# Six of 12.5 column blocks of an edge projection move from one stage to two others

## The reference, cut to what matters

```
x = x + L0_gnn(norm(x), src, dst, ...)          # stages gat_*: attention sums over edges
x = x + L0_ffn(norm(x), ...)                    # stages one_*: one of 32 experts a node
x = x + L1_gnn(norm(x), edge_attr_256, ...)     # stages edge_*

L1_gnn:  msg = (node_feats[src] + edge_feats) @ W1.T + b1
         s   = msg @ W4.T + b4 + (node_feats @ W5.T + b5)[dst]     # 8 heads
```

## Time and profile before

| | |
|---|---|
| median of 3 runs | 5361.3 us (5359.38 to 5363.87) |
| the profiled execution | 5358.89 us, its span 5357.1 us |
| mean granted TensorE clock | 0.835 of full speed |
| busy share of the span | PE 66%, DVE 55%, POOL 31%, ACT 17% |
| moved by DMA | 749.97 MB, mean 140 GB/s |

### The profile page before, as it was taken

How to read it: one execution, slowest core, us unless ns; L and a number is a source line. 1 busy time by engine, 2 the same in 40 slices (tenths; PEclk the granted TensorE clock), 3 DMA queues, 4 the chain that set the end, 5 groups by cost and what they waited for, 6 DMA issues and landing times. The chain is left out here.

```text
span 5357.1 us, 65064 instructions
## 1 busy us (share of the span) xinstructions
PE 3536.3 (66%) x17025; PEld 2564.0 (48%) x17039; DVE 2953.5 (55%) x6866; ACT 918.5 (17%) x2005; POOL 1660.0 (31%) x1548
## 2 busy tenths in 40 slices
PE   0583785364922776956679898989719636557359
PEld 0352553233511553733357686767518624345247
DVE  4696765324948977568841213030422258687657
ACT  0200001121000011204721213131304310000022
POOL 3376660224765850020010000000040246657200
PEclk9897897585965997979889898989759868879769
DMA  4276894243765970002366362626122226756200
GB/s 125 77 191 193 279 352 139 83 111 116 190 195 180 377 261 16 2 4 92 163 213 199 101 205 79 202 85 203 55 75 69 65 58 178 205 155 184 71 34 19
DMA packets 471878, 749.97 MB, mean 140 GB/s; under 512 B 70098, under 2 KB 343790, under 8 KB 467161
## 3 DMA queue, kind: packets, MB, share of 16 engines
q1 hardware_dynamic: 317021, 502.62, 28.4%
q0 software_dynamic: 82176, 177.60, 12.8%
q10 hardware_dynamic: 72436, 66.76, 3.7%
HBM read 593.67 MB, written 152.81 MB: 139 GB/s over the span
## 5 line engine op out<-in xcount | busy, mean ns | idle before, releaser
L883 PE MATMUL gin_up_sums<-gin_ring,gin_high 125*128 125x504 f32 (+1 forms) x1400 | 533.2, 381 | 32.6 <-PEq L184 32.6
L883 PE MATMUL gin_up_sums<-gin_ring,gin_low 125*128 125x504 f32 (+1 forms) x1400 | 524.4, 375 | 0.0
L863 DVE BATCH_NORM_STATS2 gin_up_stat<-gin_mlp_z 128x6 f32<-128x500 f32 (+1 forms) x112 | 70.1, 626 | 586.1 <-ACT gin_mlp_z L937 586.1
L2522 POOL IOTA two_seats_pid<- 125x1 f32 x1 | 0.1, 132 | 1145.7 <-ACTq L2519 1145.7
L883 PEld LDWEIGHTS gin_up_sums<-gin_ring,gin_high 125*128 125x128 f32 x1400 | 268.3, 192 | 74.3 <-issue 37.3
L883 PEld LDWEIGHTS gin_up_sums<-gin_ring,gin_low 125*128 125x128 f32 x1400 | 268.5, 192 | 40.5 <-issue 3.7
L3505 PE MATMUL adj_counts_part<-adj_counts_far,adj_counts_low 128*128 128x325 bf16 x1032 | 217.6, 342 | 103.3 <-DVE adj_counts_far L3481 43.3
L3134 PE MATMUL edge_sum_part<-edge_ring_rows,edge_sum_hot 128*125 x832 | 214.5, 407 | 64.2 <-DVE edge_sum_hot L1916 64.0
L3206 POOL DMA_INDIRECT edge_edge_held<-edge_table,src_e x204 | 212.6, 1042 | 105.9 <-issue 58.2
L3134 PE MATMUL loops_sum_part<-loops_ring_rows,loops_sum_hot 128*125 x832 | 212.0, 414 | 48.4 <-DVE loops_ring_rows L1495 44.6
L3134 PE MATMUL gat_sum_part<-gat_ring_rows,gat_sum_hot 128*125 x832 | 204.7, 400 | 18.8 <-issue 10.3
(11 more groups left out here) (863 smaller groups left out, 8102.1 us busy)
## 6 DMA issues: line engine op xcount, KB each, us to landing
gin_ring<-gin_adj SPq DMA_DIRECT2D x80, 1260.0 KB, 5.8
gin_ring<-gin_adj SPq DMA_DIRECT2D x60, 945.0 KB, 4.8
edge_own_rows<-edge_attr_quads_in SPq DMA_DIRECT2D x97, 512.0 KB, 12.3
gin_adj<-adj_counts_tile SPq DMA_DIRECT2D x25, 1575.0 KB
gat_sum_ef<-edge_attr_t_in SPq DMA_DIRECT2D x128, 256.0 KB
pre<-edge_edge_held ACTq DMA_DIRECT2D x204, 128.0 KB
edge_ring_rows<-pre SPq DMA_DIRECT2D x51, 512.0 KB
pre<-gat_gat_held ACTq DMA_DIRECT2D x144, 128.0 KB
```

What stands on the lines that cost most here:

```text
L863: v.bn_stats(stat[:, f, p * 6:(p + 1) * 6], z1[:, f, t0 * P:(t0 + n) * P]).then_inc(stats, 1)
L883: mm = pe.matmul(sums[h][k][:, 0:n * PC].rearrange("p (t n) -> p t n", n=PC), piece[:, t, k * 128:(k + 1) * 128], counts, start=(t == 0 an ...
L2522: pool.iota(pid[:], pattern=[[0, 1]], base=0, channel_multiplier=1, allow_small_or_imprecise_dtypes=True).then_inc(made, 1)
```

## The change

`gat_sum` keeps three of the six blocks of 512 columns and the rest: 24 full and 4 short steps in place of 48 and 4. They are spread over the 104 quads, one after three or four quads. The other 24 full steps go into a new class `OwnParts`: 12 into `one_send`, 12 into `one_back`. There SP loads a step's features (four buffers), PE multiplies, ACT takes each block of 256 columns out of PSUM and at the end writes 128 x 768 values to `edge_own`, and waits for that write. The edge features come in two arrays that are laid out so that a step is one transfer with 8 KB in one piece for each partition, in `gat_sum` too, in place of four transfers with pieces of 1 KB. The bytes stay the same.

```diff
+OWN_SENT, OWN_BACK = 3, 3
+OWN_EARLY = (OWN_SENT + OWN_BACK) * OWN_COLS // EDGE_COLS
...
+class OwnParts:
+    PLACES, HELD = RUNS // STRIPES, 4
...
+    def load(self, sp):
+
+        for n in range(self.steps):
+            if n >= self.HELD:
+                sp.wait_ge(self.projected, n - self.HELD + 1)
+            sp.dma_start(self.ef[n % self.HELD][:], self.feats[self.first * self.PLACES + n]).then_inc(self.loaded[n % self.HELD], 16)
+
+    def project(self, pe):
+
+        for n in range(self.steps):
+            b, place = n // self.PLACES, n % self.PLACES
+            low = (RUNS - 1 - place) * H
+            pe.wait_ge(self.loaded[n % self.HELD], 16 * (n // self.HELD + 1))
+            if place == 0 and b >= 2:
+                pe.wait_ge(self.put, b - 1)
+            for k in range(KD):
+                for m in range(STRIPES):
+                    mm = pe.matmul(self.bank[b % 2][m * 32:(m + 1) * 32, 0:OWN_COLS], self.g.edge_proj[:, k, low:low + 32],
+                                   self.ef[n % self.HELD][:, m, k, :], start=(place == 0 and k == 0), stop=(place == self.PLACES - 1 and k == KD - 1))
+            mm.then_inc(self.projected, 1)
+
+    def keep(self, act):
+
+        for b in range(self.count):
+            act.wait_ge(self.projected, (b + 1) * self.PLACES)
+            act.activation(self.kept[:, b, :], self.bank[b % 2][:, 0:OWN_COLS], ACT.Copy).then_inc(self.put, 1)
+        act.wait_ge(self.put, self.count)
+        lo = self.first * OWN_COLS
+        act.dma_start(self.g.edge_own[:, lo:lo + self.count * OWN_COLS], self.kept[:].rearrange("p b c -> p (b c)")).then_inc(self.out, 16)
+        act.wait_ge(self.out, 16)
...
-    QUADS, LEAD = RING // QUAD, 5
-    STEPS = LOOPS * PARTS + PLACES
...
+    QUADS, LEAD = S // QUAD, 5
+    LATE = LOOPS - OWN_EARLY
+    STEPS = LATE * PARTS + PLACES
+    end_of = [(n + 1) * QUADS // STEPS - 1 for n in range(STEPS)]
...
-                    for m in range(STRIPES):
-                        first = (m * PLACES + place) * RUN + b * EDGE_COLS + lo
-                        sp.dma_start(ef[n % HELD][:, m, :, 0:cols], ef_v[:, :, first:first + cols]).then_inc(ef_in[n % HELD], 16)
+                    late = feats[:, first:first + STRIPES * KD * cols].rearrange("p (m k c) -> p m k c", m=STRIPES, k=KD)
+                    sp.dma_start(ef[n % HELD][:, :, :, 0:cols], late).then_inc(ef_in[n % HELD], 16)
...
                 (sent,), (before,) = st2.gathers(1, top * T)
+                own = OwnParts(g, st2, early, 0, OWN_SENT) if early is not None else None
                 with st2.block() as block:
+                    if own is not None:
+                        @block.tensor
+                        def _(pe):
+                            own.project(pe)
+
+                        @block.scalar
+                        def _(act):
+                            own.keep(act)
...
                     @block.sync
                     def _(sp):
+                        if own is not None:
+                            own.load(sp)
                         sp.wait_ge(g.weights_in, g.weights_due)
                         sp.wait_ge(sent, before + 16 * top * T)
```

More of the change, by code:

```diff
@@ L1420, in _, with __init__ @@
                         q.then(v.tensor_scalar(mean[:], mean[:], 1.0 / H, None, ALU.mult))
+class OwnParts:
+    PLACES, HELD = RUNS // STRIPES, 4
+    def __init__(self, g, st, early, first, count):
+        self.g, self.first, self.count = g, first, count
+        self.steps = count * self.PLACES
+        self.feats = early.rearrange("p (n m k c) -> n p m k c", m=STRIPES, k=KD, c=OWN_COLS)
+        self.ef = [st.sb(f"own_ef{b}", [128, STRIPES, KD, OWN_COLS]) for b in range(self.HELD)]
+        self.kept = st.sb("own_kept", [128, count, OWN_COLS])
+        self.bank = [st.ps(f"own_bank{b}", [128, 512]) for b in range(2)]
+        self.loaded = st.sems("own_loaded", self.HELD)
+        self.projected, self.put, self.out = st.sem("own_projected"), st.sem("own_put"), st.sem("own_out")
+    def load(self, sp):
[23 more added lines that the diff above has]
+        act.wait_ge(self.out, 16)
 def sum_heads(nc, g, name, ring, weight, acc, ahead, edge=None, reload=None):
@@ L1524, in quad @@
                     n = (s + j) // QUAD
-                    if edge is not None and (n + 1) % spaced(n) == 0:
-                        project(step_at(n))
+                    if edge is not None and n in step_ending:
+                        project(step_ending[n])
                 pe.sem_inc(summed, HOTS)
@@ L1545, in _ @@
                 for n in range(S // QUAD):
-                    if edge is not None and n % spaced(n) == 0:
-                        load_feats(step_at(n))
+                    if edge is not None and n in step_starting:
+                        load_feats(step_starting[n])
                     c = (n + LEAD) * QUAD
@@ L1723, in gat @@
         acc = st0.sb("acc", [P, T, D + H])
[L1724 removed]
+        sum_heads(nc, g, "gat_sum", ring, weight, acc, ahead, (A["edge_attr_late"], g.edge_own, logit))
         with Stage(nc, g, "gat_out") as st:
@@ L2579, in _, with moe @@
                 q.then(v.tensor_copy(expert_of[:], expert_f[:]))
-def moe(nc, g, name, heads, bias, w1, b1_col, w2, b2, experts, hidden, top, relu):
+def moe(nc, g, name, heads, bias, w1, b1_col, w2, b2, experts, hidden, top, relu, early=None):
     HM = min(hidden, 128)
@@ L2773, in _, with seats_back @@
                     second(s)
-def seats_back(nc, g, name, seat, share, results, top, relu):
+def seats_back(nc, g, name, seat, share, results, top, relu, early):
     PLACES = 8
@@ L2783, in seats_back, with _ @@
         rows_in, before = st.gathers(PLACES, [len(order[j::PLACES]) for j in range(PLACES)])
+        own = OwnParts(g, st, early, OWN_SENT, OWN_BACK) if early is not None else None
         with st.block() as block:
+            if own is not None:
+                @block.sync
+                def _(sp):
+                    own.load(sp)
+                @block.tensor
+                def _(pe):
+                    own.project(pe)
+                @block.scalar
+                def _(act):
+                    own.keep(act)
             @block.gpsimd
@@ L3640, with by_steps @@
 LAYERS = (gat, moe_one, edge_gat, moe_all, gin, moe_two, gat_loops, ffn_top)
+def by_steps(by_run, first, last, part):
+    steps = [by_run[:, place, :, :, lo:lo + part].reshape(128, -1) for lo in range(first, last, part) for place in range(RUNS // STRIPES)]
+    return np.ascontiguousarray(np.concatenate(steps, 1))
 def laid_out(inputs):
```

44 lines of the change are left out of this document (23 added, 21 removed).

## The result

The changed kernel takes 5345.07 us (median of 6 runs, 5338.52 to 5346.65), the kernel before on the same chip 5360.52 us (6 runs, 5354.58 to 5363.87). The ratio is 0.9969 with a 95% interval of 0.9959 to 0.998. Executions of one kernel came in a fast and a slower state; ratios and their intervals are over the fast ones alone, the medians over all. The change is a gain of 15 us (of 20 forecast); the time is 4 us above the forecast of 5341 us.

What follows compares the result with a forecast made beforehand. PE (266 of 303 us) plus DMA engines bound gat_sum, POOL's train after the change. Terms -36.9 + 8.7 + 7.8 = -20.4 us gave 5341 us; forecast 5333 to 5352 (0.65), 8-in-10 range 5331 to 5355.

Steps and rivals of the forecast that it cites:

- gat_sum becomes a stage like loops_sum, 266.2 us: In gat_sum, POOL's gathers become the limit once 24 full steps leave; 303.1 falls to 266.2 us, gain 36.9.
- The signs named for it: In gat_sum: DMA share 0.8 to 0.9, POOL's train about 230 us, few waits for PE, DVE waiting for gathers.
- the 5.4 us added to the 260.8 of `loops_sum`: In gat_sum: 2.2 us for two late short steps, 1.7 for the last write, 1.5 for slower gathers.
- the 1.5 us for slower gathers: In gat_sum, rows land later with DMA engines busy about 0.85 instead of 0.59; chosen between 0 and 5 us.
- The cap by POOL's train: In gat_sum, POOL's 260.8 us as in loops_sum limits the stage, above PE's 233 and DMA's about 202.
- the DMA engines put some 30 more on top: In gat_sum before the change, PE alone needs 266 of 303 us; DMA engines add some 30.
- one_send +8.7: In one_send, 12 loads end at 1047.6, then a tail; the stage ends at 1053.4 against 1044.69, 8.7 us longer.
- The tail behind the loads: In one_send, last step, copy, issue, 2.4 us write and semaphores take 5.0 us, plus 0.8 for the barrier.
- one_back +7.8: In one_back, loads end at 1211.0; gathers landing later are covered by 8 places; stage 7.8 us longer.
- One of the prediction's own signs of being wrong: In one_send and one_back, POOL's transfers standing further apart than 1.49 us would put its train behind the loads.
- The rule on row spacing: In one_send and one_back, rows 196,608 bytes apart may collide and halve the load rate; kernel 5410 us, chance 0.07.
- The hidden case: Rival: moved work in one_send and one_back is hidden or nearly, each growing by 5 us; 5334 us, chance 0.12.

Runs made afterwards that it cites:

- move_only: Changed kernel, but gat_sum's steps load by four transfers in 1 KB pieces as before; second chip, 5604.7 us, ratio 0.9994 to before, gat_sum 321.1 us.
- sent2_back0: Changed kernel with 8 steps moved to one_send, none to one_back, 40 full steps staying in gat_sum; 5327.72 us, ratio 0.9939 to the kernel before.
- places16: Changed kernel with 16 places instead of 8 for gathered rows in one_back; 5341.23 us, ratio 0.9967 to the kernel before, one_back 55.0 us.
- loads_first: Changed kernel, but POOL's gathers in one_back wait until PE has done all twelve steps; second chip, 5611.67 us, no ratio, one_back 78.8 us.
- send2_back2_16_again: Changed kernel with 8 steps each in one_send and one_back and 16 gather places, repeated on the third chip; 5703.62 us, no ratio.
- six traces in the first table: First-chip traces of the kernel before (5359.84 us, 17 runs), the changed kernel and four follow-up kernels, 5327.72 to 5348.48 us.

## Why the prediction was right, and where it was not

The time lies within the forecast of 5333 to 5352 us. That is not all merit: one step, that of `one_back`, was wrong by 8.9 us, and 5.4 us of smaller misses the other way happened to cancel part of it.

**gat_sum becomes a stage like loops_sum, 266.2 us.** 264.3. The signs named for it are there: DMA share 0.79 (0.8 to 0.9 forecast), a train of 228 us with 1.8 us of waits for PE, DVE waiting for gathers. Of the 5.4 us added to the 260.8 of `loops_sum`, 3.5 came, all of it behind the last gather (26.4 us in place of 22.8); the 1.5 us for slower gathers did not. The cap by POOL's train was the sound step of the prediction. What it did not see is how much of that gain needs no move: it read the earlier trace rows as "the DMA engines put some 30 more on top" of PE's count and took that away by the bytes that move. The higher rate it used only for the bytes left (its 353 GB/s is the mean of all queues in 700 to 800 us before, which no row of it shows), never to ask what the layout does with all the work in place, although it had the rates, 321 against 359 GB/s, from the earlier trace rows. The layout alone gives 22.1 of the 38.8 us. That the move alone would have given all 38.8 is what the prediction implies; the 221 us of `move_only` speak for it, and no run here decides it.

**one_send +8.7.** +6.1. The size is near, the path is another. Loads and POOL's transfers together were to take 45.0 us from SP's first issue, with the loads last. Together they took about 46 (966.05 to about 1012), but the last step began after 37.9 (1003.92), since the queue ran at 400 GB/s beside the scatters:

```profile
q1 hardware_dynamic: 1728, 12.58, 78.7%
q0 software_dynamic: 2476, 2.48, 20.1%
```

That is 12.58 MB in 40 us x 0.787, and 2.48 of POOL's 3.2 MB; the rest came behind, though POOL's last scatter starts at 1002.83. The tail behind the loads was to be 5.8 us and was 10.2: the write of 384 KB, issued at 1006.34, shares the engines with the last scatters, and `one_ffn` starts at 1014.09. The queues from 1006 to 1014.1, then from 1010 to 1014:

```profile
q0 software_dynamic: 724, 0.75, 36.4%
q10 hardware_dynamic: 144, 0.39, 17.0%
...
q10 hardware_dynamic: 81, 0.21, 13.2%
q0 software_dynamic: 64, 0.07, 5.2%
```

Both have nothing left from about 1012 on. So the write took some 6 us, not the 2.4 estimated by size, and the last scatters landed no earlier, 9 us after POOL's last start (before the change the stage ended 5.2 us after it). Which of the two held the stage is not shown; without the write it would hardly have been shorter.

**one_back +7.8.** +16.7, and here a step of the mechanism failed: "POOL's gathers share the engines and land later, but 8 places and 1.5 us an issue cover 12 us". In the changed kernel the gathers landed after 16.4 us in the median and up to 21.7, about one for each load, so 8 places could not cover it. One of the prediction's own signs of being wrong is in the trace: from the tenth to the twentieth POOL's gathers start 2.3 to 4.3 us apart, not 1.5. Places 16 take 4.7 us back with twelve loads and 6.9 us with eight; loads ahead of the gathers run at 405 GB/s and show that neither queue is slow alone. The prediction shared the engines by bytes; the trace shows them shared by turns, 1165 packets of one queue for 1165 of the other. The Trainium skill says so ("DMA: Bandwidth & Descriptors", Queues, rings and completion order): an engine goes round its queues and drains a whole packet of about 9 to 17 descriptors from one before the next. The trace agrees in kind: the profile's packets are equal in number, with pieces of 8 KB a gather lands per load (3.69 us), and with pieces of 2 KB the gathers keep POOL's 1.5 us and the loads fall behind. How many of them one turn has, no row shows.

**The rule on row spacing.** The prediction gave it a small chance; it is not at work at 196,608 bytes: 405 GB/s alone, 400 beside scatters. Nor at 65,536 bytes, the row of `sent2_back0`: there the loads beside the scatters, in 980 to 992, run at 4.23 / (12 x 0.873) = 0.404 MB per us of engine time:

```profile
q1 hardware_dynamic: 586, 4.23, 87.3%
```

In no run are the features' rows further apart than the 204,800 bytes of before.

**Rivals.** The hidden case is false for twelve loads and true for eight, which the prediction's own sum allowed: 45 us x 0.73 = 33 us free against 33.5 needed, with a tail that nothing covers. It argued over the size given, not over the size that fits. In `one_back` eight are hidden only with 16 places.

## What to carry to other kernels

Before moving transfers into a stage with free DMA time, count what fits: here 8 MiB beside 25 indirect transfers cost nothing (beside the gathers 2 us at most with 16 places, 9 with 8) and 12 MiB cost 6 to 17 us. Ask of each queue how large its pieces are, not only how many bytes it has: where both had work they were served packet for packet, so large pieces on one held back gathers of small ones on the other, and then the number of buffers behind the gathers decides. When an edit changes a layout and moves work, cost the layout by itself where the work stays; it may hold most of the gain.

## What the runs showed of the hardware

**With work in both, SP's and POOL's queue were served packet for packet.** In the changed kernel 1165 and 1165 packets beside gathers, 1184 and 1185 beside scatters, with seven times as many bytes in one as in the other; with 16 places and so more gathers waiting it is the same (`places16`, 1145 to 1174: 1145 and 1147).

**Loads are slower beside gathers than beside scatters.** Engine time for one load of 1 MiB (share x window / loads): alone 0.901 x 33 / 11.6 = 2.6 us, beside scatters 0.787 x 40 / 12 = 2.6, beside gathers 3.2, by this row of the changed kernel (1135 to 1182):

```profile
q1 hardware_dynamic: 1728, 12.58, 80.8%
```

Scatters take turns from the loads and leave the engine time of a load as it is; beside gathers it is a fifth longer. Loads and gathers both read DRAM, the scatters write it, but no run separates that from other causes.

**TensorE on the second and third chip.** In `gat_sum` of `loads_first` (windows of 5 us: PE busy, records, granted clock, DMA share):

```profile
665.00:670.00 5.00, 4.82 (x33) 1.00 1.03 371
670.00:675.00 5.00, 2.38 (x9) 0.99 0.53 165
675.00:680.00 5.00, 1.79 (x3) 0.50 0.35 103
680.00:685.00 5.00, 2.09 (x5) 0.50 0.19 54
685.00:690.00 5.00, 2.71 (x7) 0.50 0.92 324
690.00:695.00 5.00, 4.88 (x29) 0.81 0.47 136
```

```profile
677.12 0.60 PE L3210 MATMUL gat_sum_part<-gat_ring_rows,gat_sum_hot 128*125 x1 [1.51 <-issue]
679.21 0.60 PE L3210 MATMUL gat_sum_part<-gat_ring_rows,gat_sum_hot 128*125 x1 [1.49 <-issue]
```

PE is running without a pause (33 records in 5 us at 2.4 GHz) when it begins to issue one matmul every 1.4 to 2.1 us with nothing to wait for, and the granted clock falls to 0.50, the 1.2 GHz level. Half the clock would make it half as fast, not a tenth (3 records in 5 us). None of the six traces in the first table has such a pause of 1.1 to 2 us with nothing to wait for; `loads_first` has 26 of them and `send2_back2_16_again` 83, in `gat_sum` and in stages before and behind it. Over `gat_sum` the same code takes 321 us here and 264 on the first chip, at a mean clock of 0.89 and 0.95. The clock looks like the consequence, since the pauses stand ahead of it; what holds the matmuls back no row shows.
